# VectorE adds the picked middle in front of the third group's searches instead of behind them

## What is computed

```python
def stage(res, cb):
    d = jnp.sum(res * res, axis=1, keepdims=True) - 2.0 * jnp.einsum('ne,ke->nk', res, cb) + jnp.sum(cb * cb, axis=1)
    idx = jnp.argmin(d, axis=1)
    q = cb[idx]
    return (res - q, q)
_, qs = jax.lax.scan(stage, x, codebooks)
quant = jnp.sum(qs, axis=0)
```

## Time and profile before

| what | value |
|---|---|
| time, median of 3 runs | 1743.99 us (1743.16 to 1745.2) |
| the profiled execution's own time | 1742.59 us |
| its span, first to last instruction | 1739.9 us |
| busy: PE / DVE / ACT / POOL | 84% / 72% / 56% / 62% of the span |
| granted TensorE clock, mean | 0.927 |
| the adds of L579 | 64, from 87.3 to 896.7 us |

### The profile page before, as it was taken

One profiled execution on the slowest core, in us unless ns is written; L12 is line 12 of the kernel. 1 busy time (PEld: TensorE's weight loads), 2 busy tenths in 40 slices (PEclk: granted clock), 3 DMA queues, 4 the chain that ended last, 5 costly groups with the idle time before them and its releaser, 6 DMA issues. The chain is left out here.

```text
span 1739.9 us, 35545 instructions
## 1 busy us (share of the span) xinstructions
PE 1454.3 (84%) x10772; PEld 646.2 (37%) x10772; DVE 1253.8 (72%) x4972; ACT 976.5 (56%) x1653; POOL 1083.2 (62%) x780
## 2 busy tenths in 40 slices
PE   3999999999999999999945999947777558686875
PEld 1333333333333333333314777716555322121211
DVE  4999999989998999999943454452222356866686
ACT  2588888878887888888832344310000024645464
POOL 3689899879888789989880232230000047867686
PEclk8799999999999999999977999969999979897977
DMA  6000000000000000000005553100000000000000
GB/s 144 8 2 9 5 9 4 10 5 2 9 4 11 4 2 9 4 2 2 2 11 116 110 106 79 34 19 0 0 0 0 23 21 1 1 1 13 1 13 24
DMA packets 16179, 35.48 MB, mean 20 GB/s; under 512 B 5636, under 2 KB 7272, under 8 KB 15996
## 3 DMA queue, kind: packets, MB, share of 16 engines
q1 hardware_dynamic: 14268, 31.96, 8.2%
q10 hardware_dynamic: 1728, 1.35, 0.3%
HBM read 9.47 MB, written 2.10 MB: 7 GB/s over the span
## 5 line engine op out<-in xcount | busy, mean ns | idle before, releaser
L549 DVE FIND_INDEX8 l_idx<-l_top,l_scored 128x8 uint32<-128x256 f32 x1024 | 412.6, 418 | 0.0
L440 POOL TENSOR_SCALAR l_onehot<-l_ib,c_iota 128x512 bf16<-128x512 f16 x256 | 399.8, 1562 | 16.3 <-ACT l_ib L387 15.3
L250 PE MATMUL ps<-l_ct_slot,l_res 32*128 32x512 f32 x2048 | 408.7, 610 | 0.0
L566 DVE CUSTOM_DVE_ANT_0 l_scored<-ps,l_gain 128x256 f32<-128x256 f32 x1024 | 379.3, 416 | 32.4 <-ACT l_gain L369 30.8
L369 ACT ACTIVATE l_gain<-ps 128x768 f32<-128x768 f32 (+1 forms) x384 | 283.5, 738 | 116.5 <-PE ps L250 116.3
L1603 POOL TENSOR_TENSOR l_isum<-l_term 128x512 f32<-128x512 f32 x160 | 205.1, 1308 | 87.3 <-DVE l_term L1701 49.6
L273 PE MATMUL ps<-l_onehot,l_cbp_slot 128*32 128x512 bf16 x3072 | 216.3, 389 | 7.9 <-POOL l_onehot L440 4.5
L244 PE MATMUL ps<-l_csq,l_row_slot 32*128 32x512 bf16 x1024 | 154.8, 396 | 21.3 <-DVE l_top L566 7.5
L735 PE MATMUL ps<-l_wc,l_xi 100*128 100x192 f32 x768 | 134.9, 334 | 31.0 <-DMA l_xi<-l_xt 31.0
L1528 ACT ACTIVATE ps<-ps,l_minus 128x512 f32<-128x512 f32 x192 | 118.2, 662 | 74.9 <-DVE l_term L1707 57.3
L250 PEld LDWEIGHTS ps<-l_ct_slot,l_res 32*128 32x128 f32 x2048 | 155.1, 194 | 11.6 <-issue 0.9
(11 more groups left out here) (158 smaller groups left out, 2010.0 us busy)
## 6 DMA issues: line engine op xcount, KB each, us to landing
l_xi<-l_xt SPq DMA_DIRECT2D x48, 384.0 KB, 7.1
X<-in_x SPq DMA_DIRECT2D x16, 128.0 KB, 7.7
out<-X SPq DMA_DIRECT2D x16, 128.0 KB, 2.2
l_ct<-in_codes_t SPq DMA_DIRECT2D x4, 448.0 KB, 13.5
l_ct_slot<-l_ct SPq DMA_DIRECT2D x7, 256.0 KB, 2.3
l_cbp_slot<-l_cbp SPq DMA_DIRECT2D x8, 96.0 KB, 1.9
l_wt<-in_l_w SPq DMA_DIRECT2D x1, 768.0 KB, 4.2
l_w_off<-in_l_w_off SPq DMA_DIRECT2D x1, 576.0 KB, 3.4
```

Source lines behind the costliest of these rows:

```text
L250: pe.matmul(ps[:, at + n - FIRST[k], :], res[rows, i, P * tt:P * (tt + 1)], ct_slot[rows, par, :], start=False, stop=True, skip_group_chec ...
L440: nc.gpsimd.tensor_scalar(onehot[:, i % 2, g, 0, :], ib16[:, i % 2, g, :], iota[:, 0:1], None, ALU.is_equal).then_inc(s_near, 1)
L549: nc.vector.max_index(idx8[:, i % 2, n, :], top[:, i % 2, n:n + 1].to_broadcast([P, 8]), scored[:, WIDE * (k % 3) + n - FIRST[k], :]).then ...
L566: nc.vector.tensor_tensor_reduce(out=scored[:, WIDE * (k % 3) + m, :], in0=ps[:, WIDE * (k % 2) + m, :PAIRED], in1=gain[:, WIDE * (k % 2) ...
```

## The change

The block with the add moves up in VectorE's `period`. Before, slot 3 was: score group 3, search group 2, add. After, it is: score group 3, add, search group 2. Nothing else changes; in the drain, where nothing is scored, the order is the same. In the first two periods there is no `mid`, so `late_quarters` is not passed by any add that exists.

```diff
-                    if k and scoring:
-                        find(i, k - 1)
-                    if isinstance(w, int) and w < 2:
-                        late_quarters(w, k)
                     if k == 3 and mid:
                         v, vi, vp = mid
                         dve.wait_ge(s_middle, START + v + 1)
                         nc.vector.tensor_tensor(res[:, vi, :], res[:, vi, :], ps[:, PICK, :],
                                                 ALU.add).then_inc(s_off, 1)
+                    if k and scoring:
+                        find(i, k - 1)
+                    if isinstance(w, int) and w < 2:
+                        late_quarters(w, k)
```

## The result

The changed kernel takes 1718.18 us in the median (1716.27 to 1718.72, 5 runs) against 1743.16 us (1741.94 to 1745.2, 5 runs) for the kernel before, measured beside it. The ratio is 0.9848 with a 95% interval of 0.9837 to 0.9859: 25 us less, faster. The forecast was 1724.2 us in a range of 1719.0 to 1733.0, so the direction was right, and the size lies 0.8 us outside the range. The profiled execution of the changed kernel took 1718.72 us, with a span of 1715.8.

The account below looks back on a forecast made before the run. PE and VectorE were both read as near their limit, with PE's side sum held by the add. 60 periods x 0.33 us = 19.8 us off 1744.0 gave 1724.2 us, range 1719 to 1733.

Parts of the forecast that it names:

- The mechanism: PE's side sum waits for VectorE's add; moving the add past three searches ends it 1.19 us earlier and frees PE.
- The add found its middle ready: VectorE's add in slot 3: the pick is seen 1.13 us before VectorE gets there, so its wait costs nothing.
- The searches that came later: VectorE's searches of group 2 come 0.59 us later, and nobody waits for them.
- the rival of the lock: GpSimd's one-hot locks VectorE's add out for 0.68 us, making the kernel slower, 1762.6 us; chance 5%.
- The neighbours: VectorE's add directly behind scoring and accumulator read: taken as no cost, 0.16 us a period at most.
- GpSimd now waits ahead of a one-hot: GpSimd's product starts 1.2 us earlier, so GpSimd waits for the pick before the first one-hot; off the path.
- 0.66 - 0.33 = 0.33 us of PE's time lost to the add: PE, spread to side sum: 0.66 us when held, 0.33 taken as unheld, so 0.33 us gained per period.
- PE's own period: PE alone, without its wait for the add, closes a period in 12.48 us.
- VectorE's own period: VectorE alone, without its waits for gains before slots 0 and 1, closes a period in 12.44 us.
- Its lower bound: Side sum starting after 0.24 us and VectorE's loop at 12.40: 24.6 us gained in all, 1719.4 us.
- the one over the top of slot 3: Loop through PE and VectorE, from scoring of slot 1 over slot 3's top, side sum and scores: 12.48 us.
- the one over the top of slot 4: Loop through PE and VectorE, from scoring of slot 1 over slot 4's top and PE's scores: 12.41 us.

Follow-up runs that it names:

- runs 1 and 2: Changed kernel with PE's side sum (first) or GpSimd's product (second) also waiting for the third search of group 2: 1742.4 us and 1716.6 us.
- run 7: Changed kernel with the third search of group 3 left out of each unit, plus a memset of the indices: 1711.9 us, ratio 0.9824.
- run 4: Changed kernel with the add moved once more, ahead of the scoring of group 3: 1746.5 us, ratio 1.0027 to the kernel before.
- The controls: Kernel before with only the extra memset of the index tile, as carried by the runs with a search left out: 1740.0 us, ratio 0.9980.
- Run 6: Kernel before with the third search of group 3, behind the add, left out of each unit, plus a memset: 1736.8 us, ratio 0.9963.
- run 8: As run 7, but PE does the side sum of slot 5 in front of the last spread: 1723.5 us, ratio 0.9894.

## What the prediction had right, and the step that failed

**The mechanism** was right, step by step. The side sum was held by the add and nothing else was worth anything (runs 1 and 2). The add found its middle ready: only the three adds of the drain wait for a pick in the changed kernel, as they did before (waits from 60 to 900 us):

```profile
DVE l_res L575 <- PE ps L273: 19.9, 3, 11.1
```

The searches that came later kept nobody waiting. The add beside GpSimd's one-hot (403.43 to 404.99) took 0.68 us against 0.66, so the rival of the lock falls as the drain's row had said; its 0.68 us of waiting did not come. The neighbours cost nothing in sum: the accumulator read and the add start together, and VectorE's period without waits is 12.414, as the distances of the kernel before add up to when the waits are taken out with their 0.02 at the hand-over behind them. GpSimd now waits ahead of a one-hot; the page names the cast as its end, but by the code this one-hot needs a cast long done and the pick of `s_middle`, which is where I had put it. The trace alone does not tell the two apart.

**The term that failed** is "0.66 - 0.33 = 0.33 us of PE's time lost to the add". I took the distance that a spread has to scores (412.71 to 413.04 in rows 3) for the distance that it has to the side sum. That is 0.23, in the changed kernel, in run 7, and in the row of the drain that I had quoted (0.24, rows 5) and used only as a bound. The side sum was held by 0.43 us, and 0.02 more went with its hand-over to the scores (1.03 against 1.01 in run 4). PE's own period is 12.37 us and not 12.48. With 12.48 for PE the changed kernel could not have reached the 12.414 us that it has.

**VectorE's own period** was the second one: 12.44 by the forecast, 12.414 measured. I took off the two stalls in front of slots 0 and 1 (0.27 and 0.10), but not that a held scoring also hands over 0.02 us later than an unheld one. With PE at 12.37 and the loop through both engines at 12.39 (run 7), VectorE alone is the longest, by 0.03. So the period fell by 0.40 instead of 0.33, and 60 x 0.40 = 24.0 us is the sum that should have stood there.

**The range** missed by 0.8 us. Its lower bound was this very case (60 x 0.41 = 24.6 us, 1719.4), and two things outside the periods lay beyond it. The sum started from a median of 1744.0, and the kernel before took 1743.2 when it was measured beside the changed one: these 0.8 us are as large as the miss. And the sum left the turns out: they gave 0.8 us more than two periods do, and the medians differ by 25.0 us. The controls show that such amounts move with matters outside of the periods.

**The loops** were right in kind. Run 4 confirms the one over the top of slot 3. Run 7 shows the one over the top of slot 4, at 12.386 us where the forecast read 12.41. Run 6 confirms that a search behind the add was on none of them while the side sum was held.

## What to carry to other kernels

Where two engines are both near 100% busy, find the wait that closes the loop, and put what releases it just ahead of its deadline: here one step of 0.39 us brought everything, two more brought 0.007 us, and one too far made it slower than it was. Take the unheld distance of a pair of instructions from a row of that very pair, however rare it is, and not from the commonest pair with the same first half. A saving far ahead of the deadline counts only after the slack of each wait in between. And a period that comes out as expected does not yet show why: in run 7 only the distance from the top to the scores told a loop through both engines from PE alone.

## What the runs showed of the hardware that I had not expected

A full 128 x 128 matmul behind a full one started earlier than one on 32 rows behind it: 0.23 against 0.33 us behind the spread, 0.96 (run 8) against 1.01 us (run 4) behind the side sum. PE's scores start 0.06 us behind the end of the top that they wait for, and a wait as short as PE's 0.03 to 0.05 us in the changed kernel shows in no list of waits. VectorE starts an addition of 128 x 512 in the same moment as the accumulator read of the scoring in front of it. And the turn of the loop is no constant: a period with a turn took 14.6 to 19.6 us over the kernels here, with plain periods of 12.4 to 12.9, and not in step with them.
